# Row sums on TensorE and squared distances on ScalarE in the closing stage of a graph network kernel

## The reference

```python
def _layernorm(x, g, b):
    mu = jnp.mean(x, axis=-1, keepdims=True)
    var = jnp.mean(jnp.square(x - mu), axis=-1, keepdims=True)
    return (x - mu) * jax.lax.rsqrt(var + EPS) * g + b
...
        x = _batchnorm(x + ff, g2[l], beta2[l])
    return _layernorm(x, ln_g, ln_b)
...
x = _layernorm(x + _L1_gnn_ref(x, edge_index, ...), axis=-1)
```

## Time and profile before

| | |
|---|---|
| time, median of 3 runs | 1683.83 us (1680.37 to 1684.9) |
| profiled execution | 1682.88 us |
| its span, first to last instruction | 1681.0 us |
| mean granted TensorE clock | 0.964 |
| closing stage, first instruction | at 1640.3 us |
| last instruction of an arithmetic engine | ends at 1677.2 us |

### The profile page before, as it was taken

One profiled execution on the slowest core, in us unless ns is written; L12 is line 12 of the kernel. 1 busy time (PEld: TensorE's weight loads), 2 busy tenths in 40 slices (PEclk: granted clock), 3 DMA queues, 4 the chain that ended last, 5 costly groups with the idle time before them and its releaser, 6 DMA issues. The chain is left out here.

```text
span 1681.0 us, 35480 instructions
## 1 busy us (share of the span) xinstructions
PE 1538.8 (92%) x14602; PEld 1417.6 (84%) x14602; DVE 1264.6 (75%) x2117; ACT 1160.5 (69%) x2089; POOL 53.9 (3%) x67
## 2 busy tenths in 40 slices
PE   7899799999997788788999999999799999999982
PEld 3788799999985777787988999999799899999982
DVE  5996899989467999996537777776842777777577
ACT  2455688888765899897537888883433788888434
POOL 0000000000000100000000100000300000000030
PEclk9999899999997999999999999999999999999995
DMA  5113222300006221112141211104030021000502
GB/s 184 54 55 105 82 75 72 132 32 2 1 1 164 109 93 63 62 63 76 38 152 56 66 53 32 33 8 137 1 121 1 10 75 32 17 14 2 129 1 61
DMA packets 58515, 103.51 MB, mean 62 GB/s; under 512 B 15569, under 2 KB 33713, under 8 KB 58352
## 3 DMA queue, kind: packets, MB, share of 16 engines
q1 hardware_dynamic: 58352, 101.22, 19.3%
HBM read 75.74 MB, written 19.21 MB: 56 GB/s over the span
## 5 line engine op out<-in xcount | busy, mean ns | idle before, releaser
L2131 DVE CUSTOM_DVE_ANT_0 probs_att<-banks,logs_or_y 125x1250 f32<-125x1250 f32 x160 | 227.3, 1457 | 124.6 <-PE banks L2015 124.1
L1028 PE MATMUL banks<-ident,probs_gat 125*125 125x125 f32 x1600 | 215.8, 285 | 44.1 <-ACT probs_gat L1132 43.4
L1028 PEld LDWEIGHTS banks<-ident,probs_gat 125*125 125x125 f32 x1600 | 196.4, 197 | 54.8 <-ACT probs_gat L1132 54.7
L1132 ACT ACTIVATE probs_gat<-probs_gat,neg_max_gat 125x1250 f32<-125x1250 f32 x160 | 214.7, 1342 | 32.7 <-DVE neg_max_gat L1301 32.3
L1301 DVE CUSTOM_DVE_ANT_0 probs_gat<-probs_gat,log_counts 125x1250 f32<-125x1250 f32 x160 | 236.7, 1480 | 0.1
L2082 ACT COPY probs_t_att<-banks 125x500 f32<-125x500 f32 x400 | 199.4, 597 | 36.3 <-PE banks L2036 36.3
L2074 ACT ACTIVATE probs_att<-probs_att,neg_max_att 125x1250 f32<-125x1250 f32 x160 | 215.7, 1372 | 9.3 <-DVE neg_max_att L2131 9.3
L2036 PE MATMUL banks<-ident,probs_att 125*125 125x125 f32 x1600 | 195.7, 278 | 3.4 <-DVE neg_max_att L2131 3.3
L2036 PEld LDWEIGHTS banks<-ident,probs_att 125*125 125x125 f32 x1600 | 180.7, 188 | 16.9 <-issue 16.4
L2045 PE MATMUL banks<-probs_t_att,v_rows 125*64 125x125 f32 x3200 | 189.0, 272 | 1.8 <-ACT probs_t_att L2082 1.8
L1039 PE MATMUL banks<-h,probs_t_gat 125*125 125x128 f32 x1600 | 188.0, 273 | 0.0
(11 more groups left out here) (258 smaller groups left out, 2868.1 us busy)
## 6 DMA issues: line engine op xcount, KB each, us to landing
a_pair<-a_src_rows SPq DMA_DIRECT2D x46, 625.0 KB, 4.8
logs_or_y<-log_rows SPq DMA_DIRECT2D x20, 546.9 KB
w_rows<-in_L_gnn_W_dram SPq DMA_DIRECT2D x12, 512.0 KB, 6.7
log_counts<-counts_fr SPq DMA_DIRECT2D x50, 122.1 KB
x_cols<-feature_cols SPq DMA_DIRECT2D x2, 2500.0 KB
logs_or_y<-x_cols SPq DMA_DIRECT2D x10, 500.0 KB, 5.2
x_rows_sb<-in_x_dram SPq DMA_DIRECT2D x1, 2240.0 KB
x_rows<-x_rows_sb SPq DMA_DIRECT2D x10, 224.0 KB
```

Source lines behind the costliest of these rows:

```text
L1028: block_t = pe.transpose(turned(u)[:, i // 2, (i % 2) * P:(i % 2 + 1) * P], probs[:, u % PROBS, i * P:(i + 1) * P], k.ident[0:P, 0:P])
L1132: act.activation(probs[:, u % PROBS], probs[:, u % PROBS], ACT.Exp, scale=-1.0, bias=neg_max[:, column(u)], accum_out=sums[:, column(u)]). ...
L2131: dve.tensor_tensor_reduce(probs[:, u % SLOTS], scores(u % 2), logs[:, t % KEPT], -1.0, -FLOOR, ALU.add, ALU.min, neg_max[:, column(u)]).t ...
```

## The change

The first norm's statistics are made in another way, and the second norm's stay as they are.

- TensorE makes each row's sum over the 512 features: after the 4 transposes of a tile come 4 products, each with the tile's columns of one chunk as the loaded operand and a column of ones as the moving one, accumulated in one element of each partition (L2610 in the changed kernel). They go to an eighth bank that all tiles share, so the ring of `z_bank` shrinks from 8 to 7. The first product of an even tile from 2 on waits until VectorE has read the sums of the group before (`mean_done`).
- VectorE turns a group's two sums into `minus_mean` (`mean_first(i)`, L2672), one instruction on 125 x 2 elements, after both tiles of the group are turned and summed.
- ScalarE reads each turned tile, squares its distance from the mean and adds up the row (`square(i)`, L2628). VectorE makes variance plus EPS of it (`spread_first(i)`, L2677).
- `bn_stats` and `bn_aggr` of the turned rows are gone from VectorE. In `gain(i)`, the reciprocal now stands between the two large operations (L2684, L2691) and not ahead of them.
- On ScalarE, `square(i+1)` stands ahead of `deviate(0, i+1)`. On VectorE, iteration i starts with `spread_first(i+1)`, `mean_first(i+2)`.

```diff
-    RING = 8
+    RING = 7
...
-        stats, moments = sb("stats", [P, 2, T, 6]), sb("moments", [P, 2, T, 2])
+        stats, moments = sb("stats", [P, T, 6]), sb("moments", [P, T, 2])
+        minus_mean, squares, apart = sb("minus_mean", [P, T]), sb("squares", [P, T]), sb("apart", [P, 2, D])
...
+        def sum_bank(t):
+            return k.psum[0:P, RING * BANK + t:RING * BANK + t + 1]
...
                 if t >= RING:
                     pe.wait_ge(gained, t - RING + 1)
                 for c in range(C):
-                    block_t = pe.transpose(z_bank(t)[:, c * 128:(c + 1) * 128], cols[:, c, t * P:(t + 1) * P], k.ident[:])
-                block_t.then_inc(turned, 1)
+                    pe.transpose(z_bank(t)[:, c * 128:(c + 1) * 128], cols[:, c, t * P:(t + 1) * P], k.ident[:])
+                if t % 2 == 0 and t >= 2:
+                    pe.wait_ge(mean_done, t // 2)
+                for c in range(C):
+                    row_sum = pe.matmul(sum_bank(t), cols[:, c, t * P:(t + 1) * P], k.ones[:], start=c == 0, stop=c == C - 1)
+                row_sum.then_inc(turned, 1)
...
+            def square(i):
+                act.wait_ge(mean_done, i + 1)
+                for t in tiles(i):
+                    if t >= 2:
+                        act.wait_ge(squared, t - 1)
+                    act.activation(apart[:, t % 2], z_bank(t), ACT.Square, bias=minus_mean[:, t:t + 1], accum_out=squares[:, t:t + 1]
+                                   ).then_inc(squared, 1)
...
             scale_cols(0)
             scale_cols(1)
+            square(0)
             deviate(0, 0)
             for i in range(GROUPS):
                 if i + 1 < GROUPS:
+                    square(i + 1)
                     deviate(0, i + 1)
...
-            def spread_out(r, i):
-                dve.wait_ge(stats_done, done["stats"])
+            def spread_out(i):
+                dve.wait_ge(stats_done, 2 * i + 2)
                 for t in tiles(i):
-                    dve.bn_aggr(moments[:, r, t], stats[:, r, t]).then_inc(moments_done, 1)
-                done["moments"] += 2
-                dve.wait_ge(moments_done, done["moments"])
-                dve.tensor_scalar(pair(spread, r, i), moments[:, r, 2 * i:2 * i + 2, 1], EPS, None, ALU.add
-                                  ).then_inc(spread_done[r], 1)
+                    dve.bn_aggr(moments[:, t], stats[:, t]).then_inc(moments_done, 1)
+                dve.wait_ge(moments_done, 2 * i + 2)
+                dve.tensor_scalar(pair(spread, 1, i), moments[:, 2 * i:2 * i + 2, 1], EPS, None, ALU.add
+                                  ).then_inc(spread_done[1], 1)
 
             def invert(r, i):
                 dve.wait_ge(deviation_done[r], i + 1)
                 dve.reciprocal(pair(inverse, r, i), pair(deviation, r, i)).then_inc(inverse_done[r], 1)
 
-            def measure_first(i):
-                for t in tiles(i):
-                    dve.wait_ge(turned, t + 1)
-                    dve.bn_stats(stats[:, 0, t, :], z_bank(t)).then_inc(stats_done, 1)
-                done["stats"] += 2
-                spread_out(0, i)
+            def mean_first(i):
+                dve.wait_ge(turned, 2 * i + 2)
+                dve.tensor_scalar(minus_mean[:, 2 * i:2 * i + 2], k.psum[0:P, RING * BANK + 2 * i:RING * BANK + 2 * i + 2], -1.0 / D, None,
+                                  ALU.mult).then_inc(mean_done, 1)
+
+            def spread_first(i):
+                dve.wait_ge(squared, 2 * i + 2)
+                dve.tensor_scalar(pair(spread, 0, i), squares[:, 2 * i:2 * i + 2], 1.0 / D, EPS, ALU.mult, ALU.add
+                                  ).then_inc(spread_done[0], 1)
 
             def gain(i):
-                invert(0, i)
                 if i == 0:
                     dve.wait_ge(k.ln_gain_loaded, 16)
                 for t in tiles(i):
-                    dve.scalar_tensor_tensor(z[:, t], z_bank(t), moments[:, 0, t, 0:1], g, ALU.subtract, ALU.mult
+                    dve.scalar_tensor_tensor(z[:, t], z_bank(t), minus_mean[:, t:t + 1], g, ALU.add, ALU.mult
                                              ).then_inc(gained, 1)
+                invert(0, i)
                 dve.wait_ge(inverse_done[0], i + 1)
                 dve.wait_ge(k.x1_loaded[i], 32)
                 for t in tiles(i):
@@ -2671,24 +2692,26 @@
                                              ).then_inc(added, 1)
                 for t in tiles(i):
                     dve.wait_ge(added, t + 1)
-                    dve.bn_stats(stats[:, 1, t, :], z[:, t]).then_inc(stats_done, 1)
-                done["stats"] += 2
-                spread_out(1, i)
+                    dve.bn_stats(stats[:, t, :], z[:, t]).then_inc(stats_done, 1)
+                spread_out(i)
 
             def centres(i):
                 invert(1, i)
                 dve.wait_ge(inverse_done[1], i + 1)
-                dve.scalar_tensor_tensor(centre[:, 2 * i:2 * i + 2], moments[:, 1, 2 * i:2 * i + 2, 0], -1.0,
+                dve.scalar_tensor_tensor(centre[:, 2 * i:2 * i + 2], moments[:, 2 * i:2 * i + 2, 0], -1.0,
                                          pair(inverse, 1, i), ALU.mult, ALU.mult).then_inc(centred, 1)
 
-            done = {"stats": 0, "moments": 0}
             for c in range(C // 2):
                 dve.tensor_scalar(cols[:, c, nodes(0)], y[:, c, nodes(0)], k.norm_scale[:, 1, c:c + 1],
                                   k.norm_shift[:, 1, c:c + 1], ALU.mult, ALU.add).then_inc(scaled_first, 1)
-            measure_first(0)
+            mean_first(0)
+            spread_first(0)
+            mean_first(1)
             for i in range(GROUPS):
                 if i + 1 < GROUPS:
-                    measure_first(i + 1)
+                    spread_first(i + 1)
+                if i + 2 < GROUPS:
+                    mean_first(i + 2)
                 if i >= 1:
                     centres(i - 1)
                 gain(i)
```

More of the change, by code:

```diff
@@ L2558, in stage_final @@
         z, x1, g = sb("z", [P, T, D]), k.x1, k.ln_gain[0:P]
-        stats, moments = sb("stats", [P, 2, T, 6]), sb("moments", [P, 2, T, 2])
+        stats, moments = sb("stats", [P, T, 6]), sb("moments", [P, T, 2])
+        minus_mean, squares, apart = sb("minus_mean", [P, T]), sb("squares", [P, T]), sb("apart", [P, 2, D])
+        mean_done, squared = k.sem("mean_done_fin"), k.sem("squared_fin")
         spread, deviation, inverse = (sb(what, [P, 2, T]) for what in ("spread", "deviation", "inverse"))
```

## The result

The changed kernel takes 1715.12 us (median of 4 runs, 1711.82 to 1716.9) against 1684.23 us before (4 runs); the ratio is 1.0186, with a 95% interval of 1.0164 to 1.0208. The prediction was 1711.8 us, in a range of 1702 to 1718.

A forecast was written before the change was run, and what follows sets the result against it. VectorE was taken to bound the closing stage. A serial chain and longer head add 31.9 us at the low clock; clock rises give back 3.0 and 0.9, leaving 28.0 slower: 1710.9, as median 1711.8 us, range 1702 to 1718.

The forecast's parts named there:

- The wait at `mean_first(i+2)`: VectorE, ahead of gain(i), waits for group i+2's turned and summed tiles: about 7.7 us each, near 30 in all.
- the ring: Serial chain per group: VectorE's gain, ScalarE's squares, VectorE's spread_first, ScalarE's scaling, TensorE's transposes and sums, VectorE again; 14.45 us.
- TensorE's burst: One group's 8 transposes and 16 product passes on TensorE at the lower clock: 5.45 us, with the start 5.50.
- the step: Time between gain's first large operations of neighbouring groups, for the first two intervals: 14.45 us where there were 6.33.
- A(2) to A(3): From gain's first large operation in group 2 to that in group 3, no group left to turn: 6.56 us.
- The head: Stage before group 0's first large gain operation, with TensorE's 48 passes for groups 0 and 1: about 15.1 us more.
- the likeliest case: Closing stage: the serial chain with the clock risen in the head, 1709 to 1714 us; chance 0.60.
- The second rival: Same serial chain, TensorE's clock low throughout because one-moving-column loads don't count as work as transposes do: 1715.7 us; chance 0.18.
- A(0): Start of gain's first large operation in group 0: near 1659 us; near 1662 if the clock did not rise.
- table load: ScalarE: roots and squares needing different tables, two loads for each of five groups, 12.8 us more, 1724.6; chance 0.03.
- The wait at `mean_first`: Rival: VectorE's wait for turned and summed tiles is covered, so 1.1 us faster, 1682.7 us; chance 0.04.
- Passes: Rival: TensorE's product passes are cheap, 0.03 us each, or all at full clock: 1701 or 1703.5 us; chance together 0.10.

The follow-up runs named there:

- mean_late: The changed kernel with mean_first(i+2) moved on VectorE from ahead of gain(i) to behind it; 1701.08 us, ratio 1.0104 to the kernel before.
- scale_ahead: The changed kernel with scale_cols one group earlier on ScalarE, VectorE's list unchanged; 1698.0 us, ratio 1.0082 to the kernel before.
- wide_ones: The changed kernel with 128 moving columns of ones instead of one in the row sums; 1712.78 us, ratio 1.0169 to the kernel before.
- hybrid: Against the kernel before: groups 2 to 4 use sums and squares, groups 0 and 1 keep bn_stats, ScalarE and VectorE reordered; 1678.76 us, ratio 0.9970.
- ordered: All work of the changed kernel in another order on ScalarE and VectorE, with the waits needed; 1684.69 us, ratio 1.0005 to the kernel before.
- one_product: The changed kernel with one product with ones per tile instead of four; 1703.77 us, ratio 1.0115 to the kernel before.
- ordered_wide: The kernel ordered with 128 moving columns of ones in place of one; 1683.69 us, ratio 0.9999 to the kernel before.

## Why the prediction held, point by point

- **The wait at `mean_first(i+2)`, in series with scaling and sums.** As forecast: 7.5 us each for groups 2 to 4, forecast 7.7, and 31.4 in all, forecast near 30. mean_late and scale_ahead cut the ring at two different links, and each stage came within 0.1 us of what had been worked out for it from the durations of the changed kernel's trace.
- **The links.** Two squares: 1.44 forecast and 1.44 in the chain. The Square itself takes 0.676 us, the value taken between the two bounds was 0.68. Scaling (2.04) and `gain` (4.61, forecast 4.59) held. TensorE's burst was 5.22 us, and the sum had 5.45; its own terms, 2.07 + 16 x 0.213, add up to 5.48. In the trace the second pass with ones of each tile starts 0.07 us after the first and not 0.21. In the first tile of a burst the next tile's transposes lose this again (0.35 us for one start), in the last tile it is kept; the rest is that the last pass ends sooner. So the step was 14.22 and not 14.45. A(2) to A(3) was 6.56, as forecast.
- **The head.** 14.6 us more, forecast 15.1 at the low clock; the same term, here the passes of six tiles, was a little too large.
- **The clock.** This is the term that failed, and with it the likeliest case, to which the prediction gave 0.60. "In the head TensorE now works on without a pause, so I expect the same rise" gave back 3.0 us, and 0.9 more for the bursts; neither came. The second rival, clock low throughout, is what happened: it had 0.18, it said 1715.7, and the median is 1715.1. As a difference it said 31.9 us and the runs say 30.9, while the forecast itself said 28.0. A(0) at 20.88 us into the stage is 1661.2 in the times of the prediction, near the 1662 that it named as the sign of this. That the median still lies in the range is owed to the range, whose upper end was drawn to take in the low clock, and not to the forecast of the clock. Its reason, that passes with one moving column don't count as work as transposes do, was tested by wide_ones: the clock had risen after 4.0 us of work with 128 columns in the same passes. Widths between 1 and 128 were not tried, so where the change of behaviour lies stays open.
- **The rule weighed against a row.** The trace decides for the loads: 16.8 us for the 80 passes with one moving column, 0.21 each at the low clock. The Trainium skill, "TensorE: Matmul & The Clock Gate", section "LDWEIGHTS (loading the stationary operand)", puts a load at its columns divided by 1.2, in ns, so 104 ns for 125 columns. The 0.11 us a pass after the rise in wide_ones are near that, the 0.21 us at the low clock are twice as long. The 25 ns of its section "Back-to-back issue gap" do not hold where each small product loads new columns. That section itself calls its table the gap of an isolated product and says that it leaves out the load, which the prediction did not weigh; the forecast by it, 17 to 18 us slower, would have been 13 us too low.
- **The rivals that fell.** No table load stands in the stage: in groups 2 to 4 the first square starts 0.11 us after the root ahead of it on ScalarE, and the root behind the squares waits 0.24 us, for VectorE's `spread_first`. The wait at `mean_first` was not covered. Passes were not cheap.
- **The idea behind the change.** VectorE's saving of 1.4 us a group was worked out as true if nothing waits. In the changed kernel it is buried under the ring; the hybrid shows it.

## What to carry to other kernels

When work moves from one engine to two others, follow one item around all the queues before pricing anything: an instruction of 0.16 us whose input hangs on the next item tied VectorE, which had bounded the stage, and two engines that had slack into one chain of 14 us. A result for a later item belongs in an engine's list behind the work that is ready, and its producer one item further ahead. And moved work need not move everywhere: the one version that beat the kernel before, the hybrid, left the first two groups, where TensorE has no lead yet, as they were.

## What the runs showed of the hardware

- A float32 product with 125 loaded columns and one moving column takes two passes, 0.21 us each at 1.2 GHz (16.8 us for 80, and 12.59 us less for 60 fewer). With 128 moving columns the passes start 0.213 us apart, and 0.11 us at 2.4 GHz (wide_ones).
- Where passes with one moving column stood among TensorE's work, its clock did not rise. It stayed at 0.50 through 10.3 us of unbroken work in the head of the changed kernel, 20.4 in scale_ahead and 25.5 in ordered. It stayed there too in the head of one_product, 5.25 us in which 16 of 24 passes are transposes. With 128 moving columns it rose after 4.0 us of work in wide_ones and 5.8 in ordered_wide, where it then stayed at 1.00 for 17 us. More arithmetic on the same loads made the stage 2.3 and 2.8 us shorter.
- A Square of 512 columns from PSUM with a bias for each partition and a sum over the row takes 0.68 us, and the read of the sum 0.195; a pair is 1.44 us from the first start to the last sum.
